# Four post-normalised stages on one core: the two-turn loop written out, the pieces of a turn in another order

## The reference

```
x = layernorm(x + L0_attn(x))   # linear attention with RoPE, 8 heads of 16, 5-tap convolution of v, output gate
x = layernorm(x + L0_ffn(x))    # x W^T plus one of four low-rank experts, weighted by its softmax weight
x = layernorm(x + L1_attn(x))   # causal softmax attention with one head of 128
x = layernorm(x + L1_ffn(x))    # 16 experts with 64 hidden units: 4 of each row's 2 best groups of 4, and a shared expert
```

## Time and profile before

| | us |
|---|---|
| median of 3 runs | 745.61 (742.17 to 746.77) |
| the profiled execution | 747.19 |
| its span, first to last instruction | 745.4 |
| PE busy | 667.1 |
| DVE busy | 607.8 |
| ACT busy | 477.9 |
| POOL busy | 323.3 |

### The profile page before, as it was taken

How to read it: one execution, slowest core, us unless ns; L and a number is a source line. 1 busy time by engine, 2 the same in 40 slices (tenths; PEclk the granted TensorE clock), 3 DMA queues, 4 the chain that set the end, 5 groups by cost and what they waited for, 6 DMA issues and landing times.

```text
span 745.4 us, 13205 instructions
## 1 busy us (share of the span) xinstructions
PE 667.1 (89%) x3632; PEld 511.7 (69%) x3632; DVE 607.8 (82%) x1892; ACT 477.9 (64%) x966; POOL 323.3 (43%) x857
## 2 busy tenths in 40 slices
PE   3565669999999999989998999989998999999994
PEld 2454657777777777767777777767776777766662
DVE  2555658898989999888988999888988899977673
ACT  3142527667777858667776868677776868576532
POOL 1325444243635363644534363644534363624311
PEclk9776869999999999999999999999999999999998
DMA  6000000000101010000101000100001000000000
GB/s 219 14 1 15 1 15 0 1 16 1 29 0 30 1 29 2 29 1 0 29 0 29 0 28 0 29 0 0 29 0 29 0 14 0 15 0 15 1 15 29
DMA packets 18678, 12.51 MB, mean 17 GB/s; under 512 B 704, under 2 KB 18240, under 8 KB 18368
## 3 DMA queue, kind: packets, MB, share of 16 engines
q1 hardware_dynamic: 18624, 11.95, 5.3%
HBM read 7.75 MB, written 4.19 MB: 16 GB/s over the span
## 4 chain that ended last, share of the span: by engine, by line
PE 56%; DVE 22%; ACT 8%; issue 7%; POOL 4%; DMA 1%; DVEq 0%; POOLq 0%; SPq 0%; ACTq 0%
PE bank L583 11%; PE bank L364 7%; PE bank L373 7%; PE bank L365 7%; PE bank L366 7%; PE bank L480 3%; ACT prob L741 2%; PE bank L443 2%; DVE wsum_e L1103 2%; DVE stats L926 2%; PE bank L550 2%; PE bank L424 2%; PE bank L468 1%; DVE gu L1115 1%; POOL moment L1221 1%
## 5 line engine op out<-in xcount | busy, mean ns | idle before, releaser
L364 PE MATMUL bank<-x3T_hi,w_hi 128*128 128x512 f32 x288 | 150.0, 521 | 9.4 <-DVE gu L1115 9.3
L583 PE MATMUL bank<-hid,whole 128*128 128x512 f32 x288 | 148.8, 599 | 1.7 <-DVE hid L1125 1.6
L776 ACT ACTIVATE silu<-bank 128x512 f32<-128x512 f32 x144 | 86.5, 601 | 89.8 <-PE bank L366 87.4
L1221 POOL TENSOR_TENSOR moment<-stats 128x4 f32<-128x4 f32 x192 | 35.1, 216 | 246.1 <-DVE stats L1049 171.2
L365 PE MATMUL bank<-x3T_lo,w_hi 128*128 128x512 f32 x288 | 114.4, 397 | 0.0
L366 PE MATMUL bank<-x3T_hi,w_lo 128*128 128x512 f32 x288 | 113.7, 395 | 0.0
L1115 DVE TENSOR_TENSOR gu<-silu,bank 128x512 f32<-128x512 f32 x128 | 87.1, 681 | 20.4 <-PE bank L366 18.2
L1125 DVE TENSOR_TENSOR hid<-gu,bank 128x512 f32<-128x512 f32 x128 | 86.4, 675 | 1.7 <-DVE gu L1115 0.2
L364 PEld LDWEIGHTS bank<-x3T_hi,w_hi 128*128 128x128 f32 x288 | 54.3, 189 | 42.7 <-DVE gu L1115 19.0
L1207 POOL TENSOR_TENSOR qk<-rope_c,rope_s 128x512 f32<-128x512 f32 x32 | 41.1, 1295 | 72.8 <-DVE rope_s L888 72.8
L365 PEld LDWEIGHTS bank<-x3T_lo,w_hi 128*128 128x128 f32 x288 | 54.5, 189 | 22.9 <-issue 17.4
(11 more groups left out here) (214 smaller groups left out, 1670.9 us busy)
## 6 DMA issues: line engine op xcount, KB each, us to landing
x_in<-x SPq DMA_DIRECT2D x16, 256.0 KB, 2.8
out<-x SPq DMA_DIRECT2D x16, 256.0 KB, 2.2
whole<-w_whole SPq DMA_DIRECT2D x1, 1198.5 KB, 5.4
w_raw<-w SPq DMA_DIRECT2D x1, 1152.0 KB
w_raw<-w SPq DMA_DIRECT2D x1, 546.0 KB, 6.6
whole<-w_whole SPq DMA_DIRECT2D x16, 32.0 KB
whole<-w_whole SPq DMA_DIRECT2D x1, 64.0 KB
```

Source lines behind the costliest of these rows:

```text
L364: mm(out, wh, mh, start=True, stop=False)
L583: mm(YB[:], whole[:, a:a + P], hid[:, c % 2], start=c == 0, stop=c == CHUNKS).then_inc(p_w2.sem, 1)
L776: fn(silu[:, c % 2], GB[:], ACT.Silu).then_inc(a_silu.sem, 1)
L1221: tt(out, in0, in1, op).then_inc(g_ln[k].sem, 1)
```

## The change

On every engine the loop is gone, and the 20 turns are written out one after another with constant semaphore values. The order of the loads and stores on SP's queue stays the same. The pieces of a turn stand in a new order on PE, ACT, DVE and POOL; no piece is added, removed or changed inside. The diff, cut to its core:

```diff
-    LEAD = 6
-    loops = (blocks - LEAD) // 2
     turns = blocks + 4
...
@@ PE: turn
                 if a: a_qk(i)
+                if d: d_down(i - 3, 0)
+                if c: c_av(i - 2)
                 if b: b_xT(i - 1)
-                if c: c_av(i - 2)
-                if d: d_down(i - 3, 0)
                 if a: a_g_(i)
+                if a: a_v_(i)
                 if b: b_small(i - 1)
+                if a: a_qT_(i)
                 if d: d_hidden(i - 3, 1 - odd, 2)
-                if a: a_v_(i)
-                if a: a_qT_(i)
+                if a: a_kv(i)
+                if d: d_hidden(i - 3, 1 - odd, 3)
                 if d: d_down(i - 3, 1)
-                if d: d_hidden(i - 3, 1 - odd, 3)
-                if a: a_kv(i)
-                if d: d_down(i - 3, 2)
                 if d: d_hidden(i - 3, 1 - odd, 4)
                 if c: r_xT(i - 2, odd)
+                if a: a_num_(i)
+                if d: d_down(i - 3, 2)
+                if d: d_hidden(i - 3, 1 - odd, 5)
+                if b: b_dnT(i - 1)
                 if d: d_down(i - 3, 3)
-                if a: a_num_(i)
-                if b: b_dnT(i - 1)
-                if d: d_hidden(i - 3, 1 - odd, 5)
                 if c: r_gate(i - 2)
                 if d: d_down(i - 3, 4)
+                if a: a_aT(i)
                 if b: b_up(i - 1)
                 if d: d_hidden(i - 3, 1 - odd, 6)
-                if a: a_aT(i)
+                if a: a_out(i)
+                if d: d_hidden(i - 3, 1 - odd, 7)
                 if d: d_down(i - 3, 5)
-                if d: d_hidden(i - 3, 1 - odd, 7)
                 if d: d_down(i - 3, 6)
                 if d: d_hidden(i - 3, 1 - odd, 8)
                 if b: c_xT(i - 1)
-                if a: a_out(i)
+                if d: d_down(i - 3, 7)
                 if b: c_project(i - 1)
-                if d: d_down(i - 3, 7)
                 if b: c_value(i - 1, 0)
+                if d: d_down(i - 3, 8)
                 if b: c_value(i - 1, 1)
-                if d: d_down(i - 3, 8)
...
-            for i in range(LEAD):
+            for i in range(turns):
                 turn(i, i % 2, i // 2)
-            with pe.Fori(0, loops) as k:
-                turn(2 * k + LEAD, 0, k + LEAD // 2)
-                turn(2 * k + LEAD + 1, 1, k + LEAD // 2)
-            for i in range(blocks, turns):
-                turn(i, i % 2)
@@ ACT: turn
+                if d: d_silu(i - 3, 0)
                 if a: x0_hi(i)
-                if d: d_silu(i - 3, 0)
...
+                if d: d_silu(i - 3, 4)
                 if b: b_exp(i - 1)
-                if d: d_silu(i - 3, 4)
...
+                if e: e_norm(i - 4)
                 if b: c_query(i - 1)
-                if e: e_norm(i - 4)
@@ DVE: turn
+                if b: a_layer_norm(i - 1)
                 if c: c_max(i - 2)
                 if d: d_gu(i - 3, 0)
                 if d: d_hid(i - 3, 0)
-                if b: a_layer_norm(i - 1)
                 if e: d_res(i - 4, odd)
...
+                if a: conv_tap(i, 4)
                 if c: r_groups(i - 2, 0)
+                if a: a_mix(i)
                 if c: r_groups(i - 2, 1)
                 if d: d_hid(i - 3, 5)
                 if b: b_res(i - 1)
                 if d: d_gu(i - 3, 6)
                 if d: d_hid(i - 3, 6)
+                if a: a_res(i, odd)
                 if c: r_groups(i - 2, 2)
-                if a: conv_tap(i, 4)
-                if a: a_mix(i)
                 if c: r_groups(i - 2, 3)
                 if d: d_gu(i - 3, 7)
+                if d: d_hid(i - 3, 7)
                 if c: r_groups(i - 2, 4)
+                if d: d_gu(i - 3, 8)
+                if c: r_combine(i - 2)
                 if second(i): split_late()
-                if d: d_hid(i - 3, 7)
-                if d: d_gu(i - 3, 8)
-                if a: a_res(i, odd)
                 if b: c_value(i - 1, 0)
                 if b: c_value(i - 1, 1)
                 if first_turn(i): fold_bias()
-                if c: r_combine(i - 2)
@@ POOL: turn
                 if c: c_shift(i - 2)
+                if e: ln_of(3, i - 4)
                 if a: a_rope(i)
                 if c: ln_of(2, i - 2)
                 if b: b_norm(i - 1)
+                if a: a_gate(i)
                 if b: ln_of(1, i - 1)
-                if a: a_gate(i)
-                if e: ln_of(3, i - 4)
                 if c: x3_lo(i - 2, odd)
```

More of the change, by code:

```diff
@@ L119, in build @@
     blocks = x_dram.shape[0] // BLOCK
-    LEAD = 6
-    loops = (blocks - LEAD) // 2
     turns = blocks + 4
-    assert blocks % 2 == 0 and loops > 0
+    assert blocks % 2 == 0
     def live(n):
@@ L347, in _ @@
                 load_after(n, n % 2)
[L348 to L353, removed]
+            for n in range(blocks):
                 store(n)
+                if n + 6 < blocks:
+                    load_after(n + 4, n % 2)
             sp.wait_ge(x_st.sem, x_st.at(blocks - 1))
@@ L789, in turn @@
                 if c: c_pT(i - 2)
+                if d: d_silu(i - 3, 1)
                 if b: copy_xT(i - 1, 1, B0)
+                if a: a_g_(i)
                 if a: a_tap0(i)
-                if d: d_silu(i - 3, 1)
-                if a: a_g_(i)
                 if b: b_small(i - 1)
-                if d: d_silu(i - 3, 2)
                 if a: a_v_(i)
                 if a: a_qT_(i)
+                if d: d_silu(i - 3, 2)
                 if d: d_silu(i - 3, 3)
                 if c: c_norm(i - 2, odd)
+                if d: d_silu(i - 3, 4)
                 if b: b_exp(i - 1)
-                if d: d_silu(i - 3, 4)
                 if c: r_hi(i - 2, odd)
+                if d: d_silu(i - 3, 5)
                 if b: b_dnT(i - 1)
-                if d: d_silu(i - 3, 5)
                 if c: r_exp(i - 2)
@@ L1143, in turn @@
                 if d: d_gu(i - 3, 1)
+                if d: d_hid(i - 3, 1)
                 if a: conv_tap(i, 1)
-                if d: d_hid(i - 3, 1)
                 if d: d_gu(i - 3, 2)
@@ L1148, in turn @@
                 if b: b_norm(i - 1, 1)
-                if a: conv_tap(i, 2)
                 if d: d_hid(i - 3, 2)
@@ L1153, in turn @@
                 if d: d_hid(i - 3, 3)
+                if a: conv_tap(i, 2)
                 if b: b_logits(i - 1)
                 if b: b_first(i - 1)
+                if d: d_gu(i - 3, 4)
                 if b: b_weigh(i - 1)
+                if d: d_hid(i - 3, 4)
                 if a: conv_tap(i, 3)
-                if d: d_gu(i - 3, 4)
                 if a: a_den(i)
+                if d: d_gu(i - 3, 5)
                 if a: a_att(i)
-                if d: d_hid(i - 3, 4)
-                if d: d_gu(i - 3, 5)
+                if a: conv_tap(i, 4)
                 if c: r_groups(i - 2, 0)
+                if a: a_mix(i)
                 if c: r_groups(i - 2, 1)
@@ L1181, in turn @@
                 if first_turn(i): fold_bias()
-                if c: r_combine(i - 2)
-            for i in range(LEAD):
-                turn(i, i % 2)
-            with dve.Fori(0, loops) as k:
-                turn(2 * k + LEAD, 0)
-                turn(2 * k + LEAD + 1, 1)
-            for i in range(blocks, turns):
+            for i in range(turns):
                 turn(i, i % 2)
@@ L1269, in turn @@
                 if b: b_norm(i - 1)
+                if a: a_gate(i)
                 if b: ln_of(1, i - 1)
-                if a: a_gate(i)
-                if e: ln_of(3, i - 4)
                 if c: x3_lo(i - 2, odd)
                 if a: ln_of(0, i)
-            for i in range(LEAD):
-                turn(i, i % 2)
-            with pool.Fori(0, loops) as k:
-                turn(2 * k + LEAD, 0)
-                turn(2 * k + LEAD + 1, 1)
-            for i in range(blocks, turns):
+            for i in range(turns):
                 turn(i, i % 2)
```

## The result

The changed kernel takes 724.18 us (median of 4 runs, 723.07 to 728.41) against 745.5: a ratio of 0.9731, 95% interval 0.9681 to 0.9781. The profiled execution took 723.07 us with a span of 721.2, 24.2 less than before.

The account below looks back on a forecast made before the run. PE was taken as the bound in turns without a jump, with DVE's loop about equal. 747.2 - 11.4 (jumps) + 1.0 (straight code) - 10.4 (order) - 2.6 (fill) = 723.8, or 722 against the median; range 713 to 735 us.

Parts of the forecast that it names:

- The jumps, -11.4: Loop on all engines: writing it out removes four jumps, each stopping DVE at `c_max` and costing 2.85 us.
- The rival in which straight code pays the stop as well: On DVE: late instruction fetch about every second turn whatever the code, so the stop remains; 732 us, chance 0.06.
- Straight code, +1.0: Ten newly written-out turns: each costs between nothing and 0.17 us more, 0 to 1.7 together, taken as +1.0 us.
- The order in the full turns, -10.4: Turns 3 to 15: the new order shortens each from 40.3 to 39.5 us, 13 x 0.8; ends -12.1 and 0.
- The two loops: In a full turn: PE alone 39.4 us, the loop through DVE 39.3 us; claimed equal within the reading.
- the two closed gaps on PE: PE's waits at `d_cT` for `comb` (0.37 us) and at `b_xT` for ACT (0.56 us) would both close.
- the list of waits that remain: DVE's loop in the new order: `c_res` for `c_av` 0.3, `gu(2)` for U 0.4, short dependency gaps 2.0 us.
- 39.37 us PE's own work: PE in a turn without a jump: 40.30 less two gaps of 0.93 us leaves 39.37 us of work.
- Fill, -2.6: Turns 1 to 3: `a_out` inside PE's wait, -0.8 in each of two turns, early `comb` -1.0; ends -4 and 0.
- The 0.8 that I put on `a_out`: PE in turns 1 and 2: `a_out` runs inside the wait for x2, saving 0.8 us in each.
- The drain, 0: Last turns: `b_dnT` behind chunk 5 gains, back-to-back chunks leave `d_gu` uncovered; set to 0, between -2 and +2 us.
- The slower rival: DVE stays late, so with `c_value` behind `r_combine` PE waits 1.8 us every turn; 754 us, chance 0.05.

Follow-up runs that it names:

- groups_late: The changed kernel with DVE's `r_groups(2)` and `r_groups(3)` moved behind `gu` and `hid` of chunk 7: 714.61 us, ratio 0.9569.
- new_loop_again: The changed kernel with the earlier loop of two turns put back on all engines, run a second time beside the changed kernel: 724.54 us.
- new_loop: The changed kernel with the earlier loop of two turns put back on all engines, first run: 726.02 us (723.33 to 730.32).
- old_combine_first: The kernel before with all turns written out, and on DVE only `r_combine` moved ahead of `c_value`: 739.06 us, ratio 0.9899.

## Why the prediction was right, and where not

**The jumps, -11.4: right.** By turns, the four jumps of the kernel with DVE's loop alone cost 42.82 + 43.45 + 42.85 + 43.54 - 4 x 40.29 = 11.5; by times 10.5 (745.46 - 735.01). They are DVE's alone, and what they cost is the fetch. The rival in which straight code pays the stop as well is out: no written-out turn has one.

**Straight code, +1.0: right in the old order, not to be seen in the new.** In the old order it is 0.11 us in each turn. In the new order PE sets the length of a turn, and the written-out turns of groups_late are no longer than the turns without a jump of its loop (39.08 against 39.25 and more).

**The order in the full turns, -10.4: the mechanism right, the size off.** The two loops, the two releases (`wsum_e`, `gscore`), the two closed gaps on PE and the foreseen waits (0.89 for `a_qk`, and 0.29 of `c_res` for `c_av`) are there as laid out. The `a_layer_norm` that I feared for is not held: its four instructions take 0.34 us each in both kernels. The turn is 39.84, not 39.5: 13 x 0.46 = 6.0 us. The step that failed is the list of waits that remain. I had both small operations short and went no further, as if the holding ended there. I had tried the moved DVE pieces against `x0_lo` and `a_gate`, and not `r_groups(3)` against `x3_lo`, the third such piece on POOL, which no longer has `a_gate` and `ln_of(3)` ahead of it since both moved ahead of `ln_of(1)`. The hold went to `cross`, and by `gu` of chunk 7 to PE, for 0.63 us. On this holding the Trainium skill (SBUF - State Buffer, Who interferes with whom) says that a DVE instruction with two SBUF inputs and a GpSimd instruction that reads SBUF contend, and, of DVE's modes with two ports, that whoever issues first keeps the ports. The traces agree on `cross`: held when POOL starts 0.013 to 0.018 us earlier (the changed kernel), 0.17 us when it starts 0.003 to 0.007 us later (new_loop_again). Closer than that the starts of the trace don't tell which came first: in new_loop `cross` was held twice at a start 0.002 us ahead of POOL's. Nor was 39.37 us PE's own work: groups_late's turn, with the same order on PE, is 39.08, and no wait is marked on PE in it. I had named a turn under 39.2 as what would prove that reading wrong. By which pieces PE gained these 0.3 us is open.

**Fill, -2.6: within its ends, but only one of its two terms holds.** In the profiled pair turn 3 starts 4.7 us earlier, of which I had foreseen 1.6. Four executions in the old order began it at 109.18, 106.87, 107.22 and 109.42 (mean 108.2), four in the changed order at 104.46, 108.59, 105.57 and 105.69 (mean 106.1): 2.1, by means of four that each spread over 2.5 us and more; the rest of the 4.7 goes with the clock that the fill happened to get. Turn 3 is 2.2 us shorter in the profiled pair, 0.46 of it as every turn: 1.8 for the 1.0 foreseen, and 1.5 in the mean of the same eight executions. This term holds: `r_combine` moved alone, in old_combine_first, shortens turn 3 by 1.3 us (41.86 to 40.58). The 0.8 that I put on `a_out` in turns 1 and 2 is no price of its own: in turn 1 the sign is the other way, and in turn 2, with `a_res` moved ahead on DVE, the place of `a_out` decides over 9 us (4.3 in turn 2 and 5.0 in turn 3).

**The drain, 0: right.** Turn 15 and the drain gained 0.5 us, which is turn 15's own share.

**The sum.** 722 + 4.4 (turns) - 1.0 (no straight code) - 1.0 (fill and turn 3: 2.1 + 1.5 for 2.6) = 724.4, against the median of 724.18. That the forecast missed by 2 us and not by 4 is partly luck, since the turns erred one way, and the straight code and the fill the other.

**The slower rival: a real mechanism, not reached.** In the changed kernel PE is late by under 0.1 us for `cv`. Put alone into the old order the step does cost more than it gives, 0.25 us in a turn, since PE's two old gaps close under its 1.08 us of wait. A slip of my sum there: with the terms given, the slower result (753 us) needs 2.3 us of wait with clock in a turn, not 1.9.

**Better than both kernels** is groups_late, 714.6 us: the same pieces, two of them behind chunk 7.

## What to carry to other kernels

When pieces are moved on VectorE or GpSimd, pair every small two-input operation that moved with every long GpSimd operation again: a hold that is freed in one place may land in another, where the queue behind it feeds the engine that sets the pace. A step of an order has no price of its own (-2.3 to +0.25 us per turn for the same swap), so a chain is followed from its producers as well as from its users. Gains of two edits add only while the bound stays the same, and an equal time of two variants may hide two effects of opposite sign, so count turns in the trace and not only medians.

## What the hardware showed that I had not expected

- Which of two operations that start within 0.02 us comes first decides over 1.1 us of one and 0.6 to 0.8 us of a turn. The same looped program had it short in all ten turns of the loop in one execution and held in seven of them in another.
- A taken jump back over the loop's body stops VectorE for 1.7 to 2.4 us in the mean. The stop ends 1.90 to 2.11 us after the start of an 8 KB fetch, in all 20 jumps. With DVE written out, no fetch starts beside the jumps of the other four engines ahead of turns 10, 12 and 14, and they cost nothing.
- From 90 us to the start of turn 3 the same program ran at a granted clock of 0.75 in one execution and 0.59 in another, and its fill was 4.1 us longer in the second.
